# Embedding the first image patches ahead of the first router rows in a fused tokenizer, scan and expert kernel

## What is computed

```python
outs = [level(x, idx, W, b, p) for p in (1, 2, 4)]        # (4, 256 / 64 / 16, 64)
h = concat([outs[0], interp(outs[1], 256), interp(outs[2], 256)]) @ Wf.T + bf
h = concat([h, txt], axis=1)                              # (4, 384, 192)
h = h + mamba(layernorm(h))       # in_proj, conv of 4, silu, softplus(dt), 16-state scan, gate, out_proj, layernorm
h = h + experts(layernorm(h))     # 8 experts of 768, the 2 best by router score, gelu
```

## Time and profile before

| | us |
|---|---|
| median of 3 runs | 431.66 |
| lowest, highest | 430.48, 434.25 |
| span of the profiled execution | 431.6 |
| TensorE busy | 379.8 (88%) |
| VectorE busy | 276.2 (64%) |
| ScalarE busy | 200.5 (46%) |
| GpSimd busy | 224.0 (52%) |
| mean granted TensorE clock | 0.941 |

### The profile page before, as it was taken

The page is one execution under the profiler, slowest core; times in us unless marked ns, Lnnn a source line. Parts: engine busy times, 40 slices in busy tenths (PEclk is TensorE's granted clock), DMA queues, the critical chain, the costliest instruction groups (busy, mean ns, idle before and its releaser), DMA issues.

```text
span 431.6 us, 6906 instructions
## 1 busy us (share of the span) xinstructions
PE 379.8 (88%) x2285; PEld 286.8 (66%) x2285; DVE 276.2 (64%) x511; ACT 200.5 (46%) x516; POOL 224.0 (52%) x166
## 2 busy tenths in 40 slices
PE   5799989979996995779968898999999999999970
PEld 4465756646564662445634486799999999999970
DVE  4605456999899998997999596643444534434400
ACT  1347447674853546734547023144444354354440
POOL 6877730564636772756637200345565554655531
PEclk9969899999989996998979997799999999999995
DMA  6401103446574875497857544433333233232224
GB/s 168 78 6 11 7 3 70 122 120 137 116 147 122 232 243 165 158 270 210 294 167 189 150 209 74 113 83 59 49 46 61 43 49 56 44 52 48 39 28 118
DMA packets 37351, 46.98 MB, mean 109 GB/s; under 512 B 9485, under 2 KB 25950, under 8 KB 36750
## 3 DMA queue, kind: packets, MB, share of 16 engines
q1 hardware_dynamic: 29998, 38.94, 32.1%
q0 software_dynamic: 7328, 7.74, 12.2%
HBM read 40.65 MB, written 7.19 MB: 111 GB/s over the span
## 4 chain that ended last, share of the span: by engine, by line
PE 60%; DVE 17%; ACT 6%; DMA 5%; POOL 5%; issue 3%; SPq 1%; POOLq 0%; DVEq 0%; ACTq 0%
PE ps L1190 15%; PE ps L1171 10%; PE ps L1179 6%; DVE w_all L1760 5%; PE ps L1005 4%; DMA w_all<-bc_dram 3%; PE ps L1053 3%; PE ps L934 3%; POOL w_all L647 3%; POOL w_all L697 2%; DVE ps L1752 2%; PE ps L1007 2%; PE ps L1161 2%; DVE stats L1586 1%; DVE h_tok L1807 1%
## 5 line engine op out<-in xcount | busy, mean ns | idle before, releaser
L697 POOL TENSOR_TENSOR w_all<-w_all 128x768 f32<-128x768 f32 x47 | 78.9, 1682 | 82.4 <-DVE w_all L1760 36.6
L722 POOL DMA_INDIRECT sum_dram<-u_cm,tok_row x31 | 50.9, 1641 | 60.5 <-ACT u_cm L1551 53.8
L1005 PE MATMUL ps<-w_all,cst 128*128 128x512 f32 x96 | 55.4, 661 | 22.9 <-POOL w_all L697 22.3
L1760 DVE TENSOR_TENSOR_SCAN w_all<-decay,ps 128x780 f32<-128x780 f32 x40 | 71.1, 1779 | 2.0 <-POOL w_all L697 0.7
L706 POOL DMA_INDIRECT dt_cm<-x_dram,tok_in x31 | 30.8, 993 | 41.0 <-DVE texi L1989 29.0
L647 POOL DMA_INDIRECT w_all<-in_pix,gidx x42 | 44.1, 1051 | 14.9 <-issue 12.5
L1536 ACT ACTIVATE u_cm<-ps,x_cm 128x128 f32<-128x128 f32 x96 | 26.5, 376 | 39.8 <-PE ps L1179 39.8
L934 PE MATMUL ps<-cst 128*128 128x256 f32 x132 | 36.5, 433 | 5.5 <-DMA cst<-in_cst 4.9
L1005 PEld LDWEIGHTS ps<-w_all,cst 128*128 128x128 f32 x96 | 16.5, 198 | 35.4 <-POOL w_all L697 30.4
L1752 DVE TENSOR_TENSOR ps<-dtu_cm,ps 128x768 f32<-128x768 f32 x40 | 38.0, 949 | 2.7 <-ACT ps L1455 2.5
L1536 ACT ACTIVATE z_cm<-ps,y_cm 128x128 f32<-128x128 f32 x90 | 24.8, 375 | 27.5 <-PE ps L1179 27.5
(11 more groups left out here) (268 smaller groups left out, 706.8 us busy)
## 6 DMA issues: line engine op xcount, KB each, us to landing
w_all<-bc_dram SPq DMA_DIRECT2D x48, 256.0 KB, 3.6
w_all<-bc_dram SPq DMA_DIRECT2D x96, 64.0 KB, 3.8
w_all<-in_w_all SPq DMA_DIRECT2D x20, 289.0 KB, 4.5
w_all<-in_w_all SPq DMA_DIRECT2D x3, 1156.0 KB, 8.9
b_wide_sb<-bc_dram SPq DMA_DIRECT2D x8, 256.0 KB, 3.9
x_dram<-x_cm SPq DMA_DIRECT2D x3, 384.0 KB, 4.6
sum_dram<-h_tok SPq DMA_DIRECT2D x3, 384.0 KB, 4.3
out<-sum_dram SPq DMA_DIRECT2D x4, 288.0 KB, 3.7
```

The lines of the kernel that those rows point to most:

```text
L697: nc.gpsimd.tensor_tensor(segments(hcs[at % 2]), inner(states[at % 2]), segments(c_sb[at % RING]), ALU.mult).then_inc(hc_rdy, 1)
L722: pool.indirect_dma_start(sum_dram, bass.IndirectOffsetOnAxis(ap=tok_row[:, i:i + 1].bitcast(U32), axis=0), y_out[:, i % 2, :], None, comp ...
L1005: nc.tensor.matmul(sums[:, 0:4 * P], ident, hcs[at % 2][:, 0:4 * P], start=False, stop=at % S == S - 1, skip_group_check=True)
L1760: v.tensor_tensor_scan(states[p], fade, drive, 0.0, ALU.mult, ALU.add).then_inc(scanned, 1)
```

## The change

On TensorE `patch_transposes(0)` goes ahead of `first_rows`, and `fine_level(0)` ahead of `interpolated(0)`; the constant products between them (2 + 7 + 1 + 1) go. The 4 constant products ahead of the first expert tile go too. The 7 behind `fused_tokens(0)` ("normed rows") stay. On ScalarE `patch_order(0)` goes right behind `coarse_rows`, `patches_transposed(0)` behind the second square, `fine_level(0)` ahead of `first_rows`, and the two scalings for `diag` behind `fused_tokens(0)`. Of the four output copies SP issues those of batches 0 and 2 and ScalarE those of batches 1 and 3; each waits for the last scatter.

```diff
--- before.py
+++ after.py
@@ -427,8 +427,8 @@
 
         RUNS = [(2 * P + K - 1, L), (0, P), (P, 2 * P + K - 1)]
         NORMS = [(0, 2), (0, 0), (0, 1), (1, 0), (2, 0), (1, 1), (2, 1), (1, 2), (2, 2)]
-        WARM = {"input weights": 10, "coarse levels": 2, "fine patches": 2, "patches": 7, "normed rows": 7, "convolution": 2,
-                "first step": 10, "last rows": 11, "slots": 20, "bias rows": 1, "first tile": 4}
+        WARM = {"input weights": 10, "coarse levels": 2,  "normed rows": 7, "convolution": 2,
+                "first step": 10, "last rows": 11, "slots": 20, "bias rows": 1}
         STEPS = NJ * S
 
         def by_pool(at):
@@ -635,7 +635,7 @@
                     .then_inc(sum_set, 16)
 
             sp.wait_ge(y_sent, 16 * MT)
-            for b in range(NB):
+            for b in range(0, NB, 2):
                 sp.dma_start(out[b], sum_dram[L * b:L * b + L, :]).then_inc(out_st, 16)
             sp.wait_ge(out_st, 16 * NB)
 
@@ -946,14 +946,10 @@
             dt_low(0)
             dt_high_and_bc(0)
             coarse_rows()
-            keep_warm(WARM["fine patches"], 0)
+            patch_transposes(0)
             first_rows()
+            fine_level(0)
             interpolated(0)
-            keep_warm(WARM["patches"], 7)
-            patch_transposes(0)
-            keep_warm(1, 7)
-            fine_level(0)
-            keep_warm(1, 7)
             fused_tokens(0)
             keep_warm(WARM["normed rows"], 0)
             norm_transposes(1)
@@ -1149,7 +1145,6 @@
                 nc.tensor.matmul(ps[:, 4 + b % 2, 256 * (b // 2):256 * (b // 2) + C],
                                  gate_t[32 * b:32 * b + E, 2 * P:3 * P], bo[32 * b:32 * b + E, :],
                                  start=True, stop=True).then_inc(bo_ps, 1)
-            keep_warm(WARM["first tile"], 6)
 
             def x_transposed(i, q):
                 p = q % 2
@@ -1388,17 +1383,17 @@
             nc.scalar.activation(a_neg[:, :, :], chan[:, :, H_A:H_A + S], ACT.Exp).then_inc(a_exp, 1)
             squares_of(0, 0, 1)
             coarse_rows()
-            squares_of(0, 1, 3)
+            patch_order(0)
+            squares_of(0, 1, 2)
+            patches_transposed(0)
+            squares_of(0, 2, 4)
+            fine_level(0)
             first_rows()
-            patch_order(0)
-            squares_of(0, 3, 4)
-            patches_transposed(0)
+            load_table(ACT.Sqrt)
+            fused_tokens(0)
             for g in range(2):
                 ins = nc.scalar.activation(diag[:, g, :], ident, ACT.Copy, scale=chan[:, g, H_D:H_D + 1])
             ins.then_inc(diag_rdy, 1)
-            fine_level(0)
-            load_table(ACT.Sqrt)
-            fused_tokens(0)
             deviation(1)
             transposed(1)
             load_table(ACT.Silu)
@@ -1551,6 +1546,9 @@
                 nc.scalar.activation(y_out[:, p, :], ps[:, 6 + p, 0:C], ACT.Copy,
                                      scale=gate_q[:, q:q + 1]).then_inc(y_rdy, 1)
             expert_loop(act, expert_tile)
+            act.wait_ge(y_sent, 16 * MT)
+            for b in range(1, NB, 2):
+                act.dma_start(out[b], sum_dram[L * b:L * b + L, :]).then_inc(out_st, 16)
 
         @block.vector
         def _(dve):
```

## The result

The changed kernel was run 20 times and the kernel before 20 times beside it. Medians: 433.14 us (430.02 to 435.66) against 432.45 us (428.08 to 440.05). The ratio of the two is given as 1.0052, with a 95% interval of 1.0031 to 1.0073: a little slower, where 0.8% faster was forecast. (The ratio leaves out executions over 1.5% above the fastest of their kernel, and with the wide scatter of the kernel before that cuts off its upper end; over all executions the means differ by 0.2 us only, 433.26 against 433.03, with standard errors of 0.3 and 0.6.) So it is half a per cent slower or the same, and in no reading 3.5 us faster.

A forecast was written before the change was run, and what follows sets the result against it. The prediction took TensorE's program order to bound the front, fillers the first expert tile's start, and SP's serial issues the end. Its terms gave 431.66 - 2.2 - 1.1 - 0.2 = 428.2 us, range 424.8 to 431.8.

The forecast's parts named there:

- router products, which took 2.53, to 42.8: Front, TensorE: router products behind the moved patch transposes would keep their old 2.53 us and end at 42.8.
- part 1: Front: moving the first patches ahead and dropping fillers among their products would gain 2.2 us, ends 5.3 and -1.3.
- fillers left behind: Front, seven fillers kept behind fused tokens: at half clock they could outlast the normed rows; 0.4 us taken as paid.
- the slower rival: Front: clock falls in the gap at 39.4, leftover fillers become the wait, time 433.2 us; chance 0.10.
- The diagonal's scalings: ScalarE, between fused copies and deviation: two scalings take 0.68 us, 0.45 hidden and 0.2 paid.
- Part 2: First expert tile without its four fillers: 3.15 us earlier, 2.05 lost to half clock, 1.1 gained; ends 2.2 and -0.25.
- Part 3: Output copies issued on two queues: issuing ends 1.2 us earlier, but landing grows; 0.2 gained, ends 1.2 and -0.6.
- The sum: Whole kernel: gains of 2.2, 1.1 and 0.2 us taken from 431.66 give 428.2.
- the base: Whole kernel: the starting time of the kernel before, taken as a median of 431.66 us.

The follow-up runs named there:

- run 20: Not a label but a count, from "run 20 times": changed kernel and kernel before, each run 20 times; medians 433.14 and 432.45 us.
- e8_no_move: Changed kernel without its moves in the front: old order, no fillers there, the rest of the change kept; ratio 0.9992 to the kernel before, mean 430.21 us.
- e4_gap: Changed kernel with four fillers put back between coarse rows and patch transposes; ratio 1.0029 to the kernel before, mean 432.17 us.
- e6_four: Changed kernel with 4 instead of 7 fillers behind the fused tokens; ratio 1.0029 to the kernel before, mean 431.19 us.
- e3_out: Kernel before with only the output copies issued on two queues; ratio 1.0005 to the kernel before.
- e9_old_front: Changed kernel with the whole front of the kernel before, order and fillers; ratio 0.9890 to the kernel before, median 429.84 us.
- e11_late_before: Kernel before with two gathers of the second half issued ahead of the first sixteen; ratio 1.0018 to the kernel before, mean 432.03 us.
- e10_late_after: Changed kernel with two gathers of the second half issued ahead of the first sixteen; ratio 1.0076 to the kernel before, mean 434.18 us.
- e5_nofill: Kernel before with its order kept and only the front's 2 + 7 + 1 + 1 fillers removed; ratio 1.0051 to the kernel before, mean 433.50 us.
- e2_tile: Kernel before with only the four fillers ahead of the first expert tile removed; ratio 0.9974 to the kernel before, mean 429.67 us.
- e1_front: Kernel before with only the front's moves and removed fillers; ratio 1.0119 to the kernel before, mean 436.81 us.
- e7_rows_late: Changed kernel with router products moved behind the fused tokens and 3 fillers after them; ratio 1.0007 to the kernel before, mean 430.99 us.

## Why the prediction was wrong

**The step that failed.** It is the term "router products, which took 2.53, to 42.8" in part 1. I had put the fall of the clock at the end of the router products. It came in the gap ahead of them, at 39.5, and they took 4.5. Fused tokens ended at 52.6 where I had 49.5, and the 3.1 us are made up of the patch transposes (0.6), the router products (2.0) and the three products behind them (7.3 instead of the 6.7 in my 49.5, so 0.6). The second step that failed is the price of the fillers left behind, below.

**Part 1, start of the patches.** Right for the execution that was profiled: ordering without a wait, transposes at 39.7 for 39.8. Wrong as a statement on the kernel: I took 39.33 for ScalarE's side and 39.27 for the gathers from one trace and never asked which of the two moves. In other executions ScalarE is 3.3 us earlier and the gathers are not. (I also misread ScalarE's idle time: between 42.45 and the wait of 5.04 us it computed one more square.) From the end of coarse rows to the normed transposes, one trace each; "moved" fronts have no fillers among the patch products:

| end of coarse rows | kernel and front | to the normed transposes |
|---|---|---|
| 34.9 | before (traced again), old front | 17.8 |
| 35.1 | `e8_no_move`, old order, no fillers | 17.3 |
| 34.9 | `e4_gap`, moved front | 21.6 |
| 34.8 | `e6_four`, moved front, 4 fillers behind | 21.9 |
| 38.1, 38.2 | before, changed | 18.0, 19.3 |
| 39.5 (and 39.7, 39.8) | `e3_out` (and `e9_old_front`, `e11_late_before`), old front | 16.1 each |
| 39.5 | `e10_late_after`, moved front, gathers delayed | 20.1 |
| 40.5 | `e5_nofill`, old order, no fillers | 19.0 |
| 40.7, 41.1 | `e2_tile` old, `e1_front` moved | 17.8, 19.3 |

Old fronts with their fillers average 17.0 over six traces. Moved ones with 7 fillers behind average 20.1 over four, but one of these has its gathers delayed and one an early head; the other two have 19.3. That is 2.3 to 3.1 us lost, where I had forecast a gain of 2.2. The table also says which part of the change costs when. With an early head it is the order (17.3 against 21.6) and the missing fillers cost nothing (17.8 against 17.3). With a late head it is the missing fillers (17.8 against 19.0) and the order costs 0.3.

**Part 1, the clock.** The fall in the gap is the slower rival, which I gave 0.10, and in the front it came out nearly to the number (52.5 and 57.4 forecast, 52.6 and 57.7 measured). Part of that is luck: its router products were 0.5 too long and its last three products 0.5 too short. Its time of 433.2 against 433.1 is luck too, since the kernel before came out at a median of 432.45 and not 431.66. My reason against the rival, that the products ahead of the gap ran at 1.00, was none: in the five other traces of the moved order too the clock fell in that gap or at most 1.3 us behind it. And the old front kept something I had not priced: in three of its six traces with fillers the clock did not fall there at all. That the three last products took 1.8 and not 2 times their full-clock length is as I had assumed; the reason that I gave for it is not tested.

**The fillers left behind.** Mechanism right, size wrong: I had put 0.4. The normed rows were ready at 56.18 and their transposes came at 57.5 to 57.7, 1.3 to 1.5 later. The trace of `e6_four` showed it.

**The diagonal's scalings.** Forecast 0.2; the deviation began 1.64 us after the statistics did, against 1.61 before, so nothing.

**Part 2.** Forecast 1.1 gained; 1.2 by the stage averages, 2.4 +- 1.0 by the mean time of `e2_tile` alone. In the changed kernel's trace the up products began 2.3 us earlier for the edit, not 3.15, since the transposes waited for the tile's fetch, and they ran at half clock for 5.3 us where I took 4.1. In the other traces without these fillers nothing waited for that fetch. That the average still comes near the forecast owes something to luck, since it rests on two traces whose clock stayed low in spite of the fillers, a case that I had not considered.

**Part 3.** Forecast 0.2, measured 0.5 +- 0.3 by the traces. Landing grew, as argued.

**The sum.** By the stage averages +3.1 - 1.2 - 0.5 = 1.4 us slower, or 0.6 with 2.3 for part 1; measured +0.2 by the means of all executions and 2.2 by the ratio. Of the 4.9 us between 428.2 and 433.14, 0.8 is the base, which I took from three executions. I had also taken the trace for a median execution; with 1.8 us on its span it belongs to one of about 433.4.

What stays open: what decides between an early and a late head (the traces show only that an early one comes with a clock that holds from 20 to 30 us), how often each occurs, and so what share of the loss each cause has; whether the gap, or the small products behind it, bring the clock down; whether the long low clock in `e7_rows_late` is typical; and why `e1_front` is slower than `e5_nofill` by 3 us in time, when their fronts differ by 0.3 in the traces.

## What to carry to other kernels

Before moving work ahead to the point where its data lands, ask of both sides of that meeting which one is fixed in time and which one wanders between executions; a move that meets a fixed transfer turns an early execution into a wait. Independent small work belongs in front of such a wait, not behind it. And fillers are two different things: between short products they kept the clock up in three of six traces here, while behind a stage that ran at half clock they grew from 3.2 to 5.1 us and became the wait that they were meant to cover.

## What the runs showed of the hardware that was not expected

The granted clock of one and the same unchanged program differs between executions: it fell at 25.7 in one trace of the kernel before and not before 39.7 in the other, which moved the end of coarse rows by 3.3 us. The spans were 431.6 and 425.1; another 2.5 of that difference lie in the scan stretch. Products with 8 to 32 columns are slower at half clock too: 20 of them took 2.5 us at 1.00 and 4.5 at 0.50. A second queue for four copies of 288 KB ended the issuing 1.2 us sooner and the last landing 0.5 +- 0.3 sooner on average.
